# One set of eight-column products for the attention's s and d, and one fp32 product that turns s into rows

## What is computed

```python
ht  = (h @ W).reshape(N, 4, 256).transpose(1, 0, 2)
src = einsum('hnd,hd->hn', ht, a_src)        # s
dst = einsum('hnd,hd->hn', ht, a_dst)        # d
e   = leaky_relu(src[:, :, None] + dst[:, None, :], 0.01) + adj_mat[None]
h_prime = einsum('hij,hjd->hid', softmax(e, axis=-1), ht).mean(axis=0)
```

## Time and profile before

| | us |
|---|---|
| median of 3 runs | 726.4 |
| lowest, highest of the runs | 725.98, 730.93 |
| the profiled execution, as a run | 727.08 |
| its span, from first to last instruction | 725.3 |
| TensorE busy | 703.7 (97%) |
| VectorE busy | 535.9 (74%) |
| ScalarE busy | 416.7 (57%) |
| GpSimd busy | 140.7 (19%) |

### The profile page before, as it was taken

One profiled execution on the slowest core, in us unless ns is written; L12 is line 12 of the kernel. 1 busy time (PEld: TensorE's weight loads), 2 busy tenths in 40 slices (PEclk: granted clock), 3 DMA queues, 4 the chain that ended last, 5 costly groups with the idle time before them and its releaser, 6 DMA issues.

```text
span 725.3 us, 17252 instructions
## 1 busy us (share of the span) xinstructions
PE 703.7 (97%) x6208; PEld 583.3 (80%) x6208; DVE 535.9 (74%) x1022; ACT 416.7 (57%) x614; POOL 140.7 (19%) x229
## 2 busy tenths in 40 slices
PE   6989999989999999999999999999999999999996
PEld 4878864478888888888888888875777778888885
DVE  5788438899898998989899898997343325874564
ACT  7545228888888879788887978644311121334000
POOL 3965322000100000000000000622021111432222
PEclk9999999999999999999999999999999999999999
DMA  9976002000303003030300303000000000000011
GB/s 322 412 278 259 0 2 60 0 1 31 59 1 71 19 30 58 29 58 0 72 14 29 58 0 59 2 1 1 1 2 2 0 1 1 1 1 1 31 45 43
DMA packets 12407, 37.26 MB, mean 51 GB/s; under 512 B 1092, under 2 KB 7108, under 8 KB 10180
## 3 DMA queue, kind: packets, MB, share of 16 engines
q1 hardware_dynamic: 9784, 28.74, 10.7%
q0 software_dynamic: 2016, 7.34, 5.4%
q10 hardware_dynamic: 560, 0.52, 0.2%
HBM read 27.13 MB, written 2.13 MB: 40 GB/s over the span
## 4 chain that ended last, share of the span: by engine, by line
PE 85%; DVE 9%; POOL 4%; issue 1%; ACT 1%; DMA 1%; POOLq 0%; DVEq 0%; SPq 0%; ACTq 0%
PE ps L502 14%; PE ps L503 14%; PE ps L637 14%; PE ps L639 14%; PE ps L638 14%; PE ps L493 7%; PE ps L593 6%; DVE ring_hl L924 2%; DVE ring_a L919 2%; PE ps L461 2%; POOL x L1023 1%; POOL ring_a L1032 1%; PE ps L486 1%; DVE x L699 1%; DVE stat L693 1%
## 5 line engine op out<-in xcount | busy, mean ns | idle before, releaser
L637 PE MATMUL ps<-arena,ring_hl 128*128 (+1 forms) x1024 | 279.6, 273 | 2.2 <-DVE ring_hl L924 2.2
L638 PE MATMUL ps<-arena,ring_hl 128*128 (+1 forms) x1024 | 279.6, 273 | 0.0
L639 PE MATMUL ps<-arena,ring_hl 128*128 (+1 forms) x1024 | 279.6, 273 | 0.0
L502 PE MATMUL ps<-arena,adj 128*128 128x256 f16 (+1 forms) x1024 | 232.5, 273 | 0.5 <-issue 0.5
L503 PE MATMUL ps<-arena,adj 128*128 128x256 f16 x1024 | 232.6, 273 | 0.0
L919 DVE SCALAR_TENSOR_TENSOR ring_a<-rho,gam,ring_a 128x1024 f32<-128x1024 f32 x128 | 163.3, 1277 | 19.5 <-ACT ring_a L401 19.5
L414 ACT ACTIVATE ring_hl<-ring_a 128x1024 f16<-128x1024 f32 x128 | 135.3, 1057 | 55.7 <-PE ps L639 36.3
L924 DVE TENSOR_TENSOR ring_hl<-ring_a,ring_hl 128x1024 f16<-128x1024 f32 x128 | 155.8, 1218 | 6.2 <-ACT ring_hl L414 6.1
L401 ACT ACTIVATE ring_a<-adj 128x1024 f32<-128x1024 bf16 x128 | 133.8, 1047 | 0.0
L502 PEld LDWEIGHTS ps<-arena,adj 128*128 (+1 forms) x1024 | 100.1, 98 | 18.5 <-issue 0.9
L637 PEld LDWEIGHTS ps<-arena,ring_hl 128*128 128x128 f16 x1024 | 100.2, 98 | 15.5 <-DVE ring_hl L924 2.7
(11 more groups left out here) (90 smaller groups left out, 607.4 us busy)
## 6 DMA issues: line engine op xcount, KB each, us to landing
arena<-in_adj SPq DMA_DIRECT2D x16, 1024.0 KB, 8.9
x<-y POOLq DMA_DIRECT2D x14, 512.0 KB, 5.3
rho<-s_scratch SPq DMA_DIRECT2D x8, 512.0 KB, 3.9
out_x<-x SPq DMA_DIRECT2D x16, 128.0 KB, 1.7
x<-in_x SPq DMA_DIRECT2D x3, 512.0 KB, 6.7
arena<-in_L_gnn_W SPq DMA_DIRECT2D x1, 1024.0 KB, 17.3
arena<-in_L_gnn_a SPq DMA_DIRECT2D x1, 1024.0 KB, 19.7
rho<-in_L_gnn_W SPq DMA_DIRECT2D x2, 512.0 KB, 10.9
```

Source lines behind the costliest of these rows:

```text
L502: nc.tensor.matmul(ps[:, bank, 0:width], lhs, pp[:, j, 0, 0:width], start=(j == 0), stop=False)
L637: nc.tensor.matmul(acc, hi, v_hi, start=(jt == 0), stop=False)
L638: nc.tensor.matmul(acc, hi, v_lo, start=False, stop=False)
L639: ins = nc.tensor.matmul(acc, lo, v_hi, start=False, stop=(jt == T - 1))
```

## The change

Each projection of k = 1 becomes one set of six products: the part of the transposed tile is held and eight columns (s and d weights) are streamed. VectorE takes all eight columns out of PSUM into `sd`, with no step of ScalarE. When all 16 tiles are there, one product with fp32 operands (`sd`'s 64 columns of s held, a 128x128 fp32 identity streamed) turns s into 64 rows of 128, for head and tile. ScalarE copies them into `srow`. The addition of the maxima and the write to DRAM work on 64 partitions by 128; a mask `head_of` picks each row's head. GpSimd makes the fp32 identity and the mask at the start.

```diff
+        ident_f = sb("ident_f", [P, P], F32)
+        head_of = sb("head_of", [P, H], F32)
-        dall = sb("dall", [P, T, H], F32)
+        sd = sb("sd", [P, 2, H, T], F32)
+        dall = sd[:, 1, :, :].rearrange("p h t -> p t h")
-        srow = r_flat[0:H, :]
+        SROWS = H * T
+        srow = r_flat[0:SROWS, 0:P]
...
-            sp.dma_start(s_dram, srow).then_inc(s_srow, 16)
+            sp.dma_start(s_dram.rearrange("h (t p) -> (h t) p", p=P), srow).then_inc(s_srow, 16)
...
-                if k == 1:
-                    nc.scalar.activation(srow[:, at(t * P, P)], b[0:H, P:2 * P], ACT.Copy, scale=1 / WS)\
-                      .then_inc(s_ph, 1)
-                    return
...
+            act.wait_ge(s_turn, 1)
+            act.wait_ge(s_wl, 3)
+            nc.scalar.activation(srow, ps[0:SROWS, 7, 0:P], ACT.Copy).then_inc(s_sr, 1)
             act.wait_ge(s_bias, 1)
...
                 if k == 1:
                     for n, (a, b, kk) in enumerate(steps):
-                        nc.tensor.matmul(bank[:, 0:H], xpart(a, kk), was[:, b, kk, 1, :],
-                                         start=(n == 0), stop=(n == len(steps) - 1))
-                    for n, (a, b, kk) in enumerate(steps):
-                        ins = nc.tensor.matmul(bank[0:H, P:2 * P], was[:, b, kk, 0, :], xpart(a, kk),
+                        ins = nc.tensor.matmul(bank[:, 0:2 * H], xpart(a, kk),
+                                               was[:, b, kk, :, :].rearrange("p s h -> p (s h)"),
                                                start=(n == 0), stop=(n == len(steps) - 1))
                     ins.then_inc(s_w, 1)
...
             values_half(2, 2, 1)
             pe.wait_ge(s_c, 2 * T)
-            values(3, 3)
+            pe.wait_ge(s_idf, 1)
+            nc.tensor.matmul(ps[0:SROWS, 7, 0:P], sd[:, 0, :, :].rearrange("p h t -> p (h t)"), ident_f[:, :],
+                             start=True, stop=True).then_inc(s_turn, 1)
+            values_half(3, 3, 0)
+            pe.wait_ge(s_sr, 1)
+            values_half(3, 3, 1)
...
-                dve.wait_ge(s_ph, t + (k * T + 1))
                 if k == 1:
-                    nc.vector.tensor_scalar(tile_of(dall, t), b[:, 0:H], 1 / WS, None, ALU.mult).then_inc(s_c, 1)
+                    dve.wait_ge(s_w, t + (k * T + 1))
+                    nc.vector.tensor_scalar(sd[:, :, :, at(t, 1)].rearrange("p s h a -> p (s h a)"), b[:, 0:2 * H],
+                                            1 / WS, None, ALU.mult).then_inc(s_c, 1)
                     return
+                dve.wait_ge(s_ph, t + ((k - (k > 1)) * T + 1))
...
-            nc.vector.tensor_tensor(dsel[0:H, :], dmb[0:H, :], ident[0:H, 0:H], ALU.mult).then_inc(s_dsel, 1)
+            dve.wait_ge(s_hs, 3)
+            nc.vector.tensor_tensor(dsel[0:SROWS, :], dmb[0:SROWS, :], head_of[0:SROWS, :], ALU.mult)\
+              .then_inc(s_dsel, 1)
-            nc.vector.reduce_sum(dcol[0:H, :], dsel[0:H, :], axis=AX.X).then_inc(s_dcol, 1)
+            nc.vector.reduce_sum(dcol[0:SROWS, :], dsel[0:SROWS, :], axis=AX.X).then_inc(s_dcol, 1)
-            dve.wait_ge(s_ph, 2 * T)
-            nc.vector.tensor_scalar(srow, srow, dcol[0:H, :], 0.0, ALU.add, ALU.max).then_inc(s_cap, 1)
+            dve.wait_ge(s_sr, 1)
+            nc.vector.tensor_scalar(srow, srow, dcol[0:SROWS, :], 0.0, ALU.add, ALU.max).then_inc(s_cap, 1)
...
+            pool.wait_ge(s_id, 1)
+            nc.gpsimd.tensor_copy(ident_f[:, :], ident[:, :]).then_inc(s_idf, 1)
+            nc.gpsimd.memset(head_of[:, :], 1.0).then_inc(s_hs, 1)
...
```

More of the change, by code:

```diff
@@ L161, in graph_stack @@
         s_srow = sem("s_srow")
+        s_idf, s_hs, s_turn, s_sr = sem("s_idf"), sem("s_hs"), sem("s_turn"), sem("s_sr")
         ld_rho = [sem(f"ld_rho{i}") for i in range(2)]
@@ L326, in one @@
                     take_t(k, t, u)
-                    take_p(k, t, u)
+                    if k != 1:
+                        take_p(k, t, u)
                 tiles(act, first, T, one)
@@ L358, in _ @@
                 take_t(1, t, t % R)
-                if t == 0:
-                    act.wait_ge(s_wl, 3)
-                take_p(1, t, t % R)
                 if t in casts_after:
@@ L1017, in _ @@
             nc.gpsimd.memset(capv[:, :], LCAP).then_inc(s_nh, 1)
+            pool.wait_ge(s_id, 1)
+            nc.gpsimd.tensor_copy(ident_f[:, :], ident[:, :]).then_inc(s_idf, 1)
+            nc.gpsimd.memset(head_of[:, :], 1.0).then_inc(s_hs, 1)
+            pool.wait_ge(s_hs, 1)
+            nc.gpsimd.affine_select(out=head_of[:, :], in_=head_of[:, :], compare_op=ALU.is_ge, fill=0.0, base=0,
+                                    pattern=[[-T, H]], channel_multiplier=1).then_inc(s_hs, 1)
+            pool.wait_ge(s_hs, 2)
+            nc.gpsimd.affine_select(out=head_of[:, :], in_=head_of[:, :], compare_op=ALU.is_ge, fill=0.0, base=T - 1,
+                                    pattern=[[T, H]], channel_multiplier=-1).then_inc(s_hs, 1)
             pool.wait_ge(s_nh, 3)
```

## The result

The changed kernel took 736.19 us (median of 4 runs, 734.53 to 737.83) beside 726.66 for the kernel before: a ratio of 1.0124, with a 95% interval of 1.0102 to 1.0146. It is slower by 1.2%, where 718.9 was forecast.

What follows compares the result with a forecast made beforehand. TensorE, busy 97% of the span, was taken as the bound. Savings of 0.40 + 7.00 + 0.49 less 0.3 and 0.1 made 7.5 us: profiled 727.08 to 719.6, median forecast 718.9 us, range 717.7 to 721.4.

Steps and rivals of the forecast that it cites:

- edits at nothing: GpSimd's added start operations, the write of `srow` in 64 pieces, VectorE's takes and the adjacency casts: claimed to cost nothing.
- The slower rival: Behind the last projection: the fp32 product delays ScalarE's exponentials; kernel slower only if it takes above 8.0 us; chance 0.02.
- A projection costs 0.15 afterwards: TensorE's projection of one tile: six products 0.025 us apart take 0.15 us instead of 0.65, saving 0.50.
- the two long steps: Steps of 0.095 and 0.15 us before and after line 486's products, where held columns change from 128 to 4 and back.
- The rival in which they stay: Projections: long steps belong to small products in general, so a tile saves only 0.335 us; 721.4 us; chance 0.12.
- Tiles 1 to 14 save 7.00, less 0.3 for addresses: TensorE's projections: 14 tiles save 0.50 us each; address work for the eight inside the loop costs 0.3 in all.
- the loop keeps its pace: Projections 1 to 10 bring nothing because another engine's cast or take comes due; 723.9 us; chance 0.04.
- Tile 0, 0.40: Tile 0's projection at half clock: about 0.8 us shorter, filled by other products at half speed, so 0.40 saved.
- Tile 15's transpose, 0.1: TensorE waits some 0.1 us for the input of tile 15's transpose, since the projections before it get shorter.
- Behind the last projection, -0.49: From the last projection to TensorE's next values: exponentials start at 2.33 us, `betw` follows at 3.38 instead of 3.87, 0.49 saved.
- A second stretch at half clock: Rival: moved events let an interruption of TensorE bring another half-clock stretch, costing 1.7 us; 720.6 us; chance 0.14.

Runs made afterwards that it cites:

- the two runs with extra products: Changed kernel without padding, with six unread products put back per projection, holding 4 columns in one run and 128 in the other: 730.25 and 725.43 us.
- the padded kernel: Changed kernel with 40 idle instructions (80 already satisfied waits) in front of TensorE's first instruction: 720.73 us, ratio 0.9907 to the kernel before.
- the run without the reduction: Changed kernel with 40 idle instructions in front on TensorE, and GpSimd's maximum over the partitions replaced by a copy: 719.63 us, one run.

## Why the prediction was wrong

It was wrong in its sign, by a cost that had no place in it.

*What was not in the sum.* The step that failed is "edits at nothing": under it I looked at what each engine does, and the removal of instructions from TensorE's program stood in the sum at nothing, without a reason. With 157 instructions fewer in front of it, the attention's loop reaches over one block more than TensorE keeps, and pays 15.2 us at two jumps back: 11.2 us of standing still (2.06, 4.39, 1.70, 3.10) and the rest at half clock and in coming back to pace. The sign that could have been read beforehand was there: the kernel before has 33 packets of instructions on q8, none between 258.6 and 441.7, a loop that is kept. And the Trainium skill's section on instruction fetch (Runtime: NRT & Kernel Launch) warns of a taken branch whose target is not in the store, and says that the fetch must end before the work goes on. It would have been a rival with a chance of its own. What that section says of two blocks that are kept is not what TensorE does here (seven stay); the run decides.

*The slower rival.* I gave it to the fp32 product, at 0.02. The product was over 0.43 us after its start, against 0.48 allowed with a change of form ahead of it. The kernel got slower by something else, so that this rival named the right direction by luck.

*A projection costs 0.15 afterwards.* Right, to the third decimal: 0.151 in tiles 1 and 2. Eight columns step as four, and the two long steps went. The rival in which they stay, at 0.12, is out by the two runs with extra products.

*Tiles 1 to 14 save 7.00, less 0.3 for addresses.* From the first projection to the sixteenth the padded kernel saves 4.97 + 2.01 = 6.98 us over fifteen projections. Forecast were 0.40 + 7.00 less 0.3 and 0.1, so 7.0, with tile 0 at half clock; with tile 0 at full clock, as in this pair, it would be 7.1. So this part of the sum held, in part because errors cancel: a whole tile got shorter by 0.513 (4.453 to 3.940) and not by 0.50. The addresses cost 0.17 in tiles 8 to 10 and nothing in the others, half of what was allowed, and those three cost 0.69 before, 0.04 more than the tile that I had taken for all. What was missed is tile 4: 0.37 in the projection and 0.2 in its late start. That is the rival "the loop keeps its pace" in one tile out of ten: a take of VectorE behind 2.82 us of other work came due. I had weighed VectorE's 17.8 free us over the whole stretch, and it is busy in lumps.

*Tile 0, 0.40.* Whether TensorE's clock falls after its 2.25 us wait near 46 us differs from one execution to the next: it did in four of the twelve profiles (before at 47.30, and three of the experiments), each time for 3.41 us. At full clock tile 0's projection saves 0.65 - 0.15 = 0.50 us. At half clock it went from 1.01 us to 0.21 (in the run without the reduction), 0.80 as I had read it; that half of this is a gain is an argument that no pair of runs tests.

*Tile 15's transpose, 0.1.* It came 0.02 late: less than allowed, and too small to matter.

*Behind the last projection, -0.49.* The padded kernel has +0.58. A second step that failed is that the biases, "ready earlier by the 0.72 that line 486 and ScalarE's copy took, gain nothing: the copy has taken their place". It let the reduction start as soon as its input is there. Of GpSimd's 6.7 us of idle time in front of it, 5.7 were preparation, which the view of that line shows as two instructions long before the reduction itself. The size is 1.07 us in this pair; without the reduction the stretch is 5.60 and not 6.94.

*A second stretch at half clock.* It came, and for a reason that the rival did not have: the stops made it.

The sum with the measured terms: 6.98 - 0.58 = 6.4 us, which is what the padded kernel gains by stages, and 6.2 in its time (720.73 against 726.97 for the kernel before, measured beside it). That is still 1.3 less than the 7.5 forecast. With the 15.2 the sum gives a loss of 8.8 us; the medians differ by 9.5, and the 0.7 between them is within what executions of the changed kernel differ by (734.53 to 737.83 us).

## What to carry to other kernels

An edit on the engine with a long loop moves that loop in its instruction store. Count the loop's instructions in blocks, and look at the instruction queue's packets: if none come after the first round, the loop is kept, and an edit in front of it, be it one that removes work, can end that; if they come in each round, a few idle instructions before it may be worth more than the edit. Where an idle time before a library operation of GpSimd ends with its input, look for its change of configuration before you count on starting it earlier. And a share of free time says nothing of one due time: check the engine's queue at the place where the shortened work will ask for it.

## What the runs showed of the hardware

TensorE keeps a loop of 1648 instructions over its rounds when it lies in seven blocks of 16 KB, and fetches all of it in each round when it lies in eight (blocks counted with the Trainium skill's 256 instructions each). TensorE then stands still at a jump back for 2.1 to 2.2 us where the loop begins in the middle of a block, and for 4.8 to 7.0 us in all where it begins near a block's end; each was followed by 3.4 to 10.2 us at half clock. The step from small products on 128 held columns to products on 4 costs 0.07 us, the way back 0.10. Products with 4 and with 8 streamed columns start 0.025 us apart. An fp32 product with 64 held and 128 streamed columns shows as two and takes TensorE 0.36 us in all. The change of GpSimd's configuration before a reduction over partitions keeps the reduction back by 5.5 to 5.9 us, and it goes on before the input is there. A small product in a loop whose addresses are not worked out ahead starts some 0.1 us behind its address operation: six of them took 0.39 to 0.57 us instead of 0.15.
